# A two-layer graph network on one core: node rows stored by ScalarE's queue, the edge step and the last stage put in another order

## The reference

```python
edge_index = jnp.stack([src, dst])
x = _layernorm(x + _L0_gnn_ref(x, edge_index, node_vec, ...), axis=-1)
x = _layernorm(x + _L1_gnn_ref(x, edge_index, edge_weight, ...), axis=-1)
# layer 0, in short
mean_neighbor = segment_sum(x[col], row) / max(deg, 1)
h_mean = (x + mean_neighbor) * 0.5 @ W_mean + b_mean
h_concat = concatenate([x @ W_ego + b_ego, mean_neighbor @ W_nb + b_nb])
gate = sigmoid(gate_weight * node_vec + gate_bias)
out0 = (1 - gate) * h_mean + gate * h_concat
# layer 1, four heads
feats = relu(x @ w1 + b1) @ w2 + b2                      # 256 -> 256 -> 64
hid = relu(concatenate([feats[row], feats[col], elem]) @ a1 + ab1)
w = exp(leaky_relu(hid @ a2 + ab2) - max)
out1 = segment_sum(w * feats[col], row) / (segment_sum(w, row) + 1e-10)
```

## Time and profile before

| | |
|---|---|
| median of 3 runs | 3639.89 us (3639.58 to 3644.17) |
| the profiled execution's own time | 3619.23 us |
| its span, first to last instruction | 3617.5 us |
| mean granted TensorE clock | 0.951 |
| PE, DVE, ACT, POOL busy in the span | 87%, 73%, 51%, 49% |
| node stage, tiles | 45 to 1431 us |
| edge step, in full flow | 1466 to 3244 us |
| last stage | 3261 to 3617.5 us |

### The profile page before, as it was taken

The page is one execution under the profiler, slowest core; times in us unless marked ns, Lnnn a source line. Parts: engine busy times, 40 slices in busy tenths (PEclk is TensorE's granted clock), DMA queues, the critical chain, the costliest instruction groups (busy, mean ns, idle before and its releaser), DMA issues. The chain is left out here.

```text
span 3617.5 us, 57511 instructions
## 1 busy us (share of the span) xinstructions
PE 3155.7 (87%) x15761; PEld 2191.4 (61%) x15761; DVE 2649.3 (73%) x8931; ACT 1849.6 (51%) x4206; POOL 1772.2 (49%) x1691
## 2 busy tenths in 40 slices
PE   6777878878889896799999999999999999995765
PEld 3444555545555554577777777777777777772333
DVE  7776766664444445588888888888888888877876
ACT  3454655555555555344444444444444444434765
POOL 2555465646666662544444444444444444403665
PEclk9998989999999998899999999999999999997898
DMA  5777887665556555433333333333333333315775
GB/s 156 256 243 263 300 273 263 208 207 194 200 189 205 198 202 192 125 117 116 115 116 116 116 116 117 114 117 114 115 116 116 116 115 117 116 42 173 229 228 170
DMA packets 289095, 597.09 MB, mean 165 GB/s; under 512 B 41326, under 2 KB 198810, under 8 KB 288950
## 3 DMA queue, kind: packets, MB, share of 16 engines
q1 hardware_dynamic: 206662, 360.13, 29.8%
q0 software_dynamic: 75744, 232.45, 20.2%
q10 hardware_dynamic: 6544, 2.89, 0.3%
HBM read 287.39 MB, written 322.05 MB: 168 GB/s over the span
## 5 line engine op out<-in xcount | busy, mean ns | idle before, releaser
L1207 POOL TENSOR_TENSOR u_hc<-u_hc 128x1536 f32<-128x1536 f32 x98 | 270.4, 2759 | 768.6 <-DVE u_h L1317 749.2
L1027 PE MATMUL bank<-w_node,xT 128*128 128x384 f32 x1564 | 600.8, 514 | 14.5 <-ACT bank L627 14.0
L1429 PE MATMUL bank<-xh,w1h 128*128 128x512 f32 x1568 | 538.0, 424 | 19.3 <-DVE xl L1346 14.5
L1259 ACT ACTIVATE hidT<-bank,b1c 128x512 f32<-128x512 f32 x392 | 268.5, 685 | 516.6 <-PE bank L1429 508.0
L1429 PE MATMUL bank<-xh,w1l 128*128 128x512 f32 x1568 | 493.9, 396 | 0.0
L1429 PE MATMUL bank<-xl,w1h 128*128 128x512 f32 x1568 | 493.4, 396 | 0.0
L1340 DVE TENSOR_SCALAR hidT<-bank,b1c 128x512 f32<-128x512 f32 x392 | 293.7, 749 | 216.0 <-PE bank L1429 211.7
L732 DVE SCALAR_TENSOR_TENSOR H<-bank,gates,X 128x256 f32<-128x256 f32 x391 | 187.3, 479 | 316.5 <-remote 164.6
L1027 PEld LDWEIGHTS bank<-w_node,xT 128*128 128x128 f32 x1564 | 295.0, 202 | 179.1 <-issue 23.1
L1443 PE MATMUL bank<-hidT,w2f 128*64 128x256 f32 x3136 | 381.7, 385 | 10.1 <-issue 10.1
L1355 DVE STREAM_TRANSPOSE feat<-catT 32x256 f32<-32x256 f32 x784 | 342.6, 437 | 17.1 <-ACT catT L1268 3.0
(11 more groups left out here) (278 smaller groups left out, 6254.8 us busy)
## 6 DMA issues: line engine op xcount, KB each, us to landing
hc_tab<-H SPq DMA_DIRECT2D x78, 960.0 KB
er<-edge_tab SPq DMA_DIRECT2D x98, 512.0 KB
X<-in_x SPq DMA_DIRECT2D x78, 640.0 KB
out_x<-O SPq DMA_DIRECT2D x78, 640.0 KB
hc_tab<-zero_row SPq DMA_DIRECT2D x10, 4032.0 KB
hc_tab<-zero_row SPq DMA_DIRECT2D x9, 3840.0 KB
edge_tab<-u_x SPq DMA_DIRECT2D x98, 256.0 KB, 2.2
edge_tab<-feat SPq DMA_DIRECT2D x98, 256.0 KB, 2.2
```

The costliest lines, as they stand in the source:

```text
L1027: ins = t_.matmul(p[:, 0:384], xT[t // 2 % XR][:, t % 2, c * P:(c + 1) * P], w_node[:, c, :], start=False, stop=c == 1, skip_group_check=True)
L1207: g.tensor_tensor(c, c, u_hc[s][:, :, MULT:MULT + 3].unsqueeze(3).to_broadcast([P, 4, 3, P]), ALU.mult).then_inc(u_scaled, 1)
L1259: a.activation(hidT[m][:, :], bank[2 + m % 2][:, :], ACT.Relu, bias=b1c[:, m:m + 1])\
L1429: ins = t_.matmul(bank[2 + m % 2][:, :], w[:, c, m * P:(m + 1) * P], xx[s][:, c, :], start=n == 0, stop=n == 5)
```

## The change

In the node stage `store_o` leaves SP. ACT issues the same stores: behind the `norm` of each fifth tile it waits for its own write and starts the transfer. In the edge step PE does both parts of `features` together in the next round instead of part 0 ahead of `hidden_7`; ACT takes its two feature copies and the seed to the head of the round and holds `relu_0` until both parts are done; DVE moves the second turning of feat to the next round, ahead of `relu_1`; SP's stores follow. In the last stage the ring has six pairs instead of four, statistics, roots, scales and norms lag one or two pairs more, one semaphore counts for each pair of zo, and the scaling of the last sum stands at the end of `add` instead of behind the loop.

```diff
@@ node stage, SP
-                def store_o(j, s):
-                    sp.wait_ge(o_done, j * TEN + (s + 1) * HALF)
-                    sp.dma_start(o_main[:, bass.ds(j * TEN + s * HALF, HALF), :], O[s][:, :, :])\
-                        .then_inc(o_out[s], 16)
@@
                 for j in range(1, ITER - 1):
                     for s in range(2):
-                        store_o(j - 1, s)
                         half(j, s, j < CLEARS)
                 for s in range(2):
-                    store_o(ITER - 2, s)
                     half(ITER - 1, s, False)
-                for s in range(2):
-                    store_o(ITER - 1, s)
@@
-                sp.wait_ge(o_done, NT + 1)
-                sp.dma_start(out[N - P:N], O[0][:, 0, :]).then_inc(o_out[0], 16)
@@ node stage, ACT, norm
                     a.activation(O[s][:, k, :], H[s][:, k, 0:D], ACT.Identity, bias=nb_s[:, i:i + 1],
                                  scale=r_s[:, i:i + 1]).then_inc(o_done, 1)
+                    if t == NT:
+                        act.wait_ge(o_done, NT + 1)
+                        for half_ in range(2):
+                            act.wait_ge(o_out[half_], 16 * ITER)
+                        act.dma_start(out[N - P:N], O[0][:, 0, :]).then_inc(o_out[0], 16)
+                    elif k == HALF - 1:
+                        act.wait_ge(o_done, t + 1)
+                        act.dma_start(o_main[:, t - k:t + 1, :], O[s][:, :, :]).then_inc(o_out[s], 16)
@@ edge step
-                skewed(sp, US, 2, [(keep_x, 0), (keep_f, 1)])
+                skewed(sp, US, 2, [(keep_f, 4), (keep_x, 0)])
@@ ACT
                 def relu(u, m):
                     act.wait_ge(w1_ready, u * 8 + (m + 1))
+                    if m == 0 and after(u, 1):
+                        act.wait_ge(w2_ready, u * 2)
@@
-                skewed(act, US, 2, [(relu_0, 2), (features_1, 3), (seed_0, 3), (root, 0), (relu_2, 2), (norm, 0),
-                                    (relu_4, 2), (seed_1, 3), (high, 1), (relu_6, 2), (features_0, 2)])
+                skewed(act, US, 2, [(seed_0, 3), (features_0, 3), (relu_0, 2), (features_1, 3), (root, 0), (relu_2, 2),
+                                    (norm, 0), (relu_4, 2), (seed_1, 3), (high, 1), (relu_6, 2)])
@@ DVE
-                skewed(dve, US, 2, [(stat, 0), (relu_1, 2), (feat_0, 3), (scale, 0), (relu_3, 2), (dots_0, 3),
-                                    (relu_5, 2), (low, 1), (dots_1, 3), (feat_1, 3), (relu_7, 2)])
+                skewed(dve, US, 2, [(stat, 0), (feat_1, 4), (relu_1, 2), (scale, 0), (feat_0, 3), (relu_3, 2),
+                                    (dots_0, 3), (relu_5, 2), (low, 1), (dots_1, 3), (relu_7, 2)])
@@ PE
                 def features(u, k):
-                    pe.wait_ge(act_hid, u * 4 + 2 * k + 2)
-                    pe.wait_ge(dve_hid, u * 4 + 2 * k + 2)
-                    if after(u, 1):
-                        pe.wait_ge(cat_ready, u * 4 + 2 * k - 2)
+                    if k == 0:
+                        pe.wait_ge(act_hid, u * 4 + 4)
+                        pe.wait_ge(dve_hid, u * 4 + 4)
+                        if after(u, 1):
+                            pe.wait_ge(cat_ready, u * 4)
@@
-                def features_1(u, s):
+                def features_0_1(u, s):
+                    features(u, 0)
                     features(u, 1)
@@
-                skewed(pe, US, 2, [(hidden_0, 1), (features_1, 2), (hidden_1, 1), (hidden_2, 1), (scores_0, 2),
+                skewed(pe, US, 2, [(hidden_0, 1), (features_0_1, 2), (hidden_1, 1), (hidden_2, 1), (scores_0, 2),
                                    (hidden_3_4, 1), (turn, 0), (hidden_5, 1), (scores_1, 2), (hidden_6, 1),
-                                   (features_0, 1), (hidden_7, 1)])
+                                   (hidden_7, 1)])
@@ last stage
-        SL = 8
-        SP2 = SL // 2
-        Z0 = 3
+        RING = 6
+        Z0 = 2
@@ ACT
-                straight(ET // 2, SP2, [(root, 2), (seed, 0), (choose, 0), (norm, 3)])
+                straight(ET // 2, RING, [(root, 3), (seed, 0), (choose, 0), (norm, 5)])
@@ DVE
-                straight(ET // 2, SP2, [(stat, 2), (weigh, 0), (aggr, 2), (scale, 3), (add, 0), (variance, 2),
-                                           (shift, 3)])
+                straight(ET // 2, RING, [(stat, 3), (weigh, 0), (aggr, 3), (scale, 4), (add, 0), (finish, 0), (variance, 3),
+                                         (shift, 4)])
```

More of the change, by code:

```diff
@@ L1531, in build @@
              "fix_var fix_sd fix_nb fix_o_ready fix_o_out").split())
-        er_in = [sem(f"er_in{s}") for s in range(SP2)]
+        er_in = [sem(f"er_in{s}") for s in range(RING)]
         z_opened, z_seeded = sem("z_opened"), sem("z_seeded")
-        zo_out = cn_out[0:SL]
-        IN0 = [(len(range(2 * q, ET, RS)) + len(range(2 * q + 1, ET, RS))) * 16 for q in range(SL)]
+        zo_out = cn_out[0:RING]
+        IN0 = [(len(range(2 * q, ET, RS)) + len(range(2 * q + 1, ET, RS))) * 16 for q in range(RING)]
         pair_rows = edge_tab.rearrange("b p d -> (b p) d")
@@ L1541, in load @@
                 def load(u, s):
-                    if after(u, SP2):
-                        sp.wait_ge(z_seeded, u - (SP2 - 1))
-                        sp.wait_ge(val_ready, u - (SP2 - 1))
+                    if u >= RING:
+                        sp.wait_ge(z_seeded, u - (RING - 1))
+                        sp.wait_ge(val_ready, u - (RING - 1))
                     sp.dma_start(er[s][:, :, :], edge_tab[bass.ds(u * 2, 2)].rearrange("b p d -> p b d"))\
                         .then_inc(er_in[s], 16)
-                straight(ET // 2, SP2, [(load, 0)])
+                straight(ET // 2, RING, [(load, 0)])
             @block.gpsimd
@@ L1562, in put @@
                     g.indirect_dma_start(out=out, out_offset=bass.IndirectOffsetOnAxis(idx_s[:, t, 3:4], 0),
-                                         in_=zo[q // 2][:, q % 2, :], in_offset=None, bounds_check=last,
-                                         oob_is_err=False).then_inc(zo_out[q], 16)
-                straight(ET, SL, [(put, 2)])
+                                         in_=zo[s][:, q, :], in_offset=None, bounds_check=last,
+                                         oob_is_err=False).then_inc(zo_out[s], 16)
+                straight(ET, 2, [(put, 0)])
                 pool.wait_ge(fo_ready, 1)
@@ L1570, in _ @@
                     .then_inc(fo_out, 16)
-                for q in range(SL):
-                    pool.wait_ge(zo_out[q], SLOTS[q] * 16 + IN0[q])
+                for s in range(RING):
+                    pool.wait_ge(zo_out[s], SLOTS[s] * 32 + IN0[s])
                 pool.wait_ge(fo_out, 16)
@@ L1655, in _ @@
                 st.done(v.tensor_reduce(fix_w[:, 0, :], w_end[:, :, :], AX.X, ALU.add))
-                st.done(v.memset(agg[SP2 - 1][:, 1, :], 0.0))
+                st.done(v.memset(agg[RING - 1][:, 1, :], 0.0))
                 st.wait()
@@ L1679, in add @@
                     dve.wait_ge(val_ready, u + 1)
-                    if after(u, SP2):
-                        dve.wait_ge(z_ready, u - (SP2 - 1))
-                        dve.wait_ge(head_used, u * 2 - 6)
+                    if u >= RING:
+                        dve.wait_ge(z_ready, u - (RING - 1))
+                        dve.wait_ge(head_used, 2 * (u - RING) + 2)
                     for k in range(2):
-                        last_ = agg[s][:, 0, :] if k else agg[(s - 1) % SP2][:, 1, :]
+                        last_ = agg[s][:, 0, :] if k else agg[(s - 1) % RING][:, 1, :]
                         if k or after(u, 1):
@@ L1732, in _ @@
                 st.wait()
-                st.done(v.tensor_tensor(fix_z[:, :], bank[2][:, 0:D], fix_z[:, :], ALU.add))
+                st.done(v.tensor_tensor(fix_z[:, :], bank[1][:, 0:D], fix_z[:, :], ALU.add))
                 st.done(v.reciprocal(fix_w[:, 1, :], fix_w[:, 0, :]))
@@ L1755, in _ @@
                 t_ = nc.tensor
-                for s in range(SP2):
+                for s in range(RING):
                     ins = t_.matmul(bank[Z0 + s][:, :], ident[:, :], bias_all[:, :], start=True, stop=True)
@@ L1769, in heads @@
                         pe.wait_ge(pick_ready, u * 2 + (k + 1))
-                        t_.matmul(bank[0][:, 0:D], pick[s % 2 * 2 + k][:, :], agg[s][:, k, :],
+                        t_.matmul(bank[0][:, 0:D], pick[u % 2 * 2 + k][:, :], agg[s][:, k, :],
                                   start=k == 0 and not after(u, 1),
@@ L1773, in heads @@
                                   skip_group_check=True).then_inc(head_used, 1)
-                straight(ET // 2, SP2, [(join, 0), (heads, 0)])
+                straight(ET // 2, RING, [(join, 0), (heads, 0)])
                 pe.wait_ge(tail_ready, 1)
-                t_.matmul(bank[2][:, 0:D], earlier_same[:, :], tail[:, :], start=True, stop=True)
-                t_.matmul(bank[1][:, 0:HEADS], earlier_same[:, :], w_sum[:, ET - 1, :], start=True, stop=True)\
```

(5 more changed lines are left out.)

55 lines of the change are left out of this document (28 added, 27 removed).

## The result

The changed kernel took 3583.07 us (median of 4 executions, 3579.78 to 3591.75) against 3639.73 us for the kernel before (4 executions, 3622.53 to 3644.17): 0.984 of the time, 95% interval 0.981 to 0.988, 57 us less. Forecast were 16 us less, 3624, range 3600 to 3660: the sign was right, the size was not, and the result lies outside the range.

What follows compares the result with a forecast made beforehand. Node stage: no engine full, handovers bound it; edge step: PE, 99% busy; last stage: DVE leads. Node +13, edge step -30, last stage +1 give -16 us: 3639.89 - 16 = 3624, range 3600 to 3660.

Steps and rivals of the forecast that it cites:

- the late rounds of the edge step: Edge step: in 26 rounds PE waits for DVE's late relu_7 ahead of the second features block, 10.7 us; 4 less taken.
- the border of a block: Edge step on PE: a lone features block's borders cost 0.29 us; joining two saves 98 x 0.29 = 28 us.
- the exposure of the stores: Node stage: share of ACT's store time that lengthens the stage, 0 to 62 us; a third taken, 13 us.
- The store costs 79 x 0.5 = 40 us of ACT time: Node stage: each of ACT's 79 stores costs 0.44 to 0.78 us of wait and issue, 0.5 taken.
- forecast -30: Edge step in all: -28 from the borders, -4 from PE's waits, +2 from the drain.
- the drain: Edge step's end: part 0 of the last step comes behind relu_7, 2 us more, once.
- feat_1 now lies ahead of relu_1 ... : 0: Edge step on DVE: hidden_3 needs relu_1's bank 2 us later than DVE's preceding work ends, so no cost.
- `relu_7` late every round (11%): Edge step rival, 11%: PE waits 0.62 us for DVE in each of 98 rounds, +38 us in all, 3678.
- the +14 of the two other stages: Forecast outside the edge step: node stage +13 us for the stores, last stage +1 us.
- Last stage, +1 (-6 to +8): Last stage, deeper ring: start about 3 us less, end 5 us more, partly hidden; +1 net.
- the ring's rival: Last stage rival, 6%: the deeper ring takes away most of DVE's 58 us of pauses, say 45; 3579.
- Sum and base: Whole kernel: +13 - 30 + 1 = -16 us, taken from the timed median 3639.89, gives 3624.

Runs made afterwards that it cites:

- the padded kernel: Kernel before with O's stores on ACT's queue and ACT normalising each fifth tile three times instead of once: ratio 1.0046, 17 us slower than the kernel before.
- set 1: Runs on the chip of 3636 against the kernel before: itself unchanged 0.9993, stores on ACT alone 1.0009, edge step's orders alone 0.9882, last stage alone 0.9993.
- a loop: Kernel before with the last stage's SP, ACT, DVE and PE orders looped over four pairs instead of written out 98 times: ratio 1.0049, 18 us slower.

## Why the prediction missed, step by step

The step that failed most is the one on the late rounds of the edge step, which the prediction put at 4 us of gain and the runs at 12; beside it the border of a block and the exposure of the stores were mis-sized.

**"The store costs 79 x 0.5 = 40 us of ACT time":** right, 0.51 to 0.6 us each, and no earlier load of X. The Trainium skill (DMA: Bandwidth & Descriptors, Issuing engines are not separate DMA queues) says that issuing from several engines saves only the issue time; the trace agrees: 338 ns on either engine, and nothing gained. **"I take a third, 13 us"** failed: 12% by the padded kernel, an estimated 5 us; +3 (-4 to +11) measured alone, 0 on the chip of 3334. The +13.8 between the two profiles, which seemed to prove it, is mostly the node stage's scatter, 22 us between profiles with SP's stores.

**"So a block's borders cost 0.09 + 0.20 = 0.29 us":** mis-sized; a round without lateness fell from 17.98 to 17.63, 0.35 us, 34 us in 98 rounds instead of 28. The prediction took the 0.10 us of the longer first pair behind a block out of the pitch, and then forgot that it belongs to the border. Joined, the block gives 0.05 back: 32 matmuls span 3.295 us from first to last start, two blocks of 16 span 1.568 each, so the seam is 0.16 instead of 0.105. 0.29 + 0.10 - 0.05 = 0.34.

**"What makes relu_5 late the rows do not show ... so I take 4 less":** this is the step that failed most in the edge step. All late rounds went in full flow, in all eight profiles of the new orders without added copies, on three chips or more: behind the first three rounds what exceeds the regular round adds up to 11.0 to 13.9 us in six profiles of the old orders on chips of 3636, and to 0.4 at most in the eight. The orders did it indirectly: `feat_1` left the place ahead of `stat`, so `stat`, and POOL's loads that wait for it, came 1.5 us sooner against PE, out of `relu_5`'s way. Putting POOL's work back by added copies brought the late rounds back. The prediction saw that DVE's and POOL's work shifts against PE, and priced it as chance. Edge step: -34 - 12 = -46, measured -43 and -48, and -47.5 between the two profiles; forecast -30. The first three rounds give 2 us more, and the drain takes 1.5 back where 2 was forecast.

**`relu_1`, "feat_1 now lies ahead of relu_1 ... : 0":** right for the whole change, but it is the merged block that hides it; alone the move costs 0.64 us a round (17.98 to 18.62).

**`relu_7` late every round (11%):** not so with `feat_1` out of the way, 0.16 us of slack against the 0.09 worked out; with `feat_1` left in the way, the merge alone waits 1.67 us a round. Two figures of this rival don't follow from its own terms: with the +14 of the two other stages in the sum, a wait of 0.30 us a round decides for slower, not 0.45, and 0.23 cancels the gain, not 0.3.

**Last stage, +1 (-6 to +8):** measured -3 and -5, both within. Over six profiles with the old ring and four with the new, on chips of 3636, first `val` to last aggregate fell from 304.1 to 299.0 in the mean (forecast -3) and the rest grew from 25.5 to 29.9 (forecast +5, part of it hidden). Together that is -0.7 us. 2.51 us a pair and the pauses stayed (28 over 0.8 us, 41 us, after; 31 with 42 us before), so the ring's rival is out.

**Sum and base:** by the runs +5 (0 to 9) - 46 - 4 = -45, measured -44 (-52 to -36). Of the 41 us between forecast and result, 16 lie in the edge step (6 in the borders, 8 in the late rounds, 2 in its start and drain), 8 in the stores and 5 in the last stage. The remaining 12 are scatter of 4 and 4 executions, which differ by some 20 us from one to the next in the node stage. The range left the miss out because it priced the late rounds with hardly any gain: even the measured -44 from its base of 3640 gives 3596, under its 3600. It also took its base for exact, as three executions agreed within 5 us; that was luck, for the 29 of set 1 lie between 3621 and 3656.

Still open: what DVE stands for behind POOL's load; what makes its pauses in the node and last stages, which one chip does not have; why the node stage scatters. No kernel here that does the whole work beats the changed one by more than its scatter: the edge step alone took 3588.9 us beside its 3593.7.

## What to carry to other kernels

When the engine that bounds a stage waits now and then for another, look at what a third engine does at that moment: an order changed for one reason moves it too, and here that was worth a quarter of the gain where it helped, and all of it where it was undone. Price a block's border with everything that differs between its first and last instruction and the regular pitch, the slow first pair included. Two edits that are only worth anything together look bad one by one, so test the pair before dropping the parts; and before reading a stage's difference between two profiles as a cost, profile the kernel before a second time.

## What the runs showed of the hardware that was not expected

- The kernel before took 3334, 3636 and 3671 us on different chips. The changed kernel has the same busy time of DVE in the node stage (831 and 830 us) and the same edge step on the first two; the difference lies in the node and last stages, the ones with a DMA share of 0.66 and 0.71, which move the same bytes at 224 and 223 GB/s on the chip of the first profile and at 273 and 271 on the fast one. In the node stage DVE's waits over 0.8 us that end "remote" or "issue" add up to 293 us for the changed kernel on the slow chip and to none on the fast one, whose node stage is 250 us shorter. PE's granted clock is lower on the slow chip too, 0.93 against 0.98 in the node stage. What is the cause and what follows is not shown; in the last stage of the kernel before, the transfers that start during DVE's pauses over 1.2 us run at 242 GB/s, against 231 over the stage, so there they don't slow down first.
- DVE's pauses at waits for its own last instruction don't come from the length of the stream: a loop kept them (32, 52 us), and on another chip they are absent (2 over 0.8 us, both ended by ACT). The Trainium skill (Runtime: NRT & Kernel Launch, Instruction fetch mechanics) says that crossing a refill boundary is mostly hidden; the loop agrees in so far as fewer fetched instructions (7 packets instead of 29) took no pause away.
- A VectorE instruction on a PSUM bank (`relu_5`) started 0.8 to 1.0 us behind the end of an indirect load's instruction on GpSimd (0.95 us long) in 167 late rounds, 0.6 to 1.1 us later than when the two are apart. It was so in about half of the rounds in which the load started 0.42 to 0.80 us ahead of the matmul that it waits for, and in full flow in none with the load 2.06 to 2.24 us ahead.
